# A two-layer graph network: the first attention's bias is added to X by the vector engine in the convolution's first 16 groups, instead of being multiplied in by the tensor engine

## What is computed

```python
xn = _layernorm(x)
x = x + gnn(xn, W, edge_index) + mix(xn, W_qkv, W_out, b_out)
# gnn: h = xn @ W; out = segment_sum(h[src] * norm, dst)
# mix: ... context = k^T v; out = (q @ context) @ W_out + b_out
```

## Time and profile before

| | |
|---|---|
| median of 3 runs | 2628.09 us |
| lowest, highest | 2627.09, 2628.97 us |
| span of the profiled execution, first to last instruction | 2779.7 us |
| the same less the median | 151.6 us |
| busy in that span: PE, PEld | 82%, 68% |
| DVE, ACT, POOL | 52%, 31%, 57% |
| gather stage, first to last gather | 138.3 to 1302.1 us |

### The profile page before, as it was taken

One profiled execution on the slowest core, in us unless ns is written; L12 is line 12 of the kernel. 1 busy time (PEld: TensorE's weight loads), 2 busy tenths in 40 slices (PEclk: granted clock), 3 DMA queues, 4 the chain that ended last, 5 costly groups with the idle time before them and its releaser, 6 DMA issues. The chain is left out here.

```text
span 2779.7 us, 48472 instructions
## 1 busy us (share of the span) xinstructions
PE 2272.5 (82%) x13041; PEld 1897.3 (68%) x13042; DVE 1437.7 (52%) x3979; ACT 857.8 (31%) x2513; POOL 1598.0 (57%) x2187
## 2 busy tenths in 40 slices
PE   7854767767677676665979999999998999996898
PEld 5633555555455554343869999978888999995798
DVE  9742534333444445336752222258876777777211
ACT  2500222222112111112623333346663434432333
POOL 4666566665666666674035555458866555552232
PEclk9977878777787787667599999999999999998899
DMA  5233233332333333332323334332221111111121
GB/s 156 98 98 89 77 88 88 87 91 78 89 91 88 89 91 90 90 94 70 127 78 104 102 124 135 106 89 87 79 68 54 45 43 42 45 43 63 29 35 31
DMA packets 138623, 227.41 MB, mean 82 GB/s; under 512 B 26651, under 2 KB 99056, under 8 KB 138546
## 3 DMA queue, kind: packets, MB, share of 16 engines
q0 software_dynamic: 56240, 142.70, 18.4%
q1 hardware_dynamic: 81186, 82.10, 8.9%
q10 hardware_dynamic: 1120, 1.71, 0.2%
HBM read 175.10 MB, written 51.30 MB: 81 GB/s over the span
## 5 line engine op out<-in xcount | busy, mean ns | idle before, releaser
L944 POOL DMA_INDIRECT all_XN<-h_table,l_srcI x782 | 774.7, 991 | 395.6 <-issue 217.0
L1145 PE MATMUL gcn_acc<-all_XN,gcn_hot 128*128 128x256 f32 x796 | 258.1, 470 | 96.0 <-DVE all_X L1036 45.3
L1145 PE MATMUL gcn_acc<-all_XN 128*128 128x256 f32 x768 | 249.5, 473 | 92.0 <-issue 41.3
L1145 PEld LDWEIGHTS gcn_acc<-all_XN,gcn_hot 128*128 128x128 f32 x796 | 178.7, 235 | 157.9 <-issue 77.3
L1145 PEld LDWEIGHTS gcn_acc<-all_XN 128*128 128x128 f32 x768 | 172.7, 236 | 149.8 <-issue 90.1
L878 ACT COPY gcn_seen_sb<-gcn_seen 128x392 f32<-128x392 f32 x98 | 47.4, 484 | 591.1 <-remote 489.6
L1836 ACT ACTIVATE moe_hidden<-moe_hid_ps,moe_b 128x128 f32<-128x128 f32 x420 | 131.2, 363 | 283.1 <-PE moe_hid_ps L1917 272.5
L1036 DVE SCALAR_TENSOR_TENSOR all_X<-gcn_acc,all_XN,all_X 128x256 f32 x392 | 170.3, 475 | 89.5 <-remote 81.5
L1917 PEld LDWEIGHTS moe_hid_ps<-moe_xst,held_held 128*128 128x128 f32 x1680 | 204.4, 193 | 11.9 <-issue 7.3
L1917 PE MATMUL moe_hid_ps<-moe_xst,held_held 128*128 128x128 f32 x1680 | 207.8, 277 | 1.9 <-DVE moe_xst L1857 1.9
L1924 PE MATMUL moe_y_ps<-held_held,moe_hidden 128*128 128x256 f32 x840 | 199.7, 381 | 0.8 <-DVE moe_y L1888 0.8
(11 more groups left out here) (431 smaller groups left out, 4737.2 us busy)
## 6 DMA issues: line engine op xcount, KB each, us to landing
held_held<-in_e_w SPq DMA_DIRECT2D x32, 512.0 KB
slots_out<-moe_y SPq DMA_DIRECT2D x105, 128.0 KB
all_XN<-h_table,l_srcI POOLq DMA_INDIRECT x782
all_X<-in_x SPq DMA_DIRECT2D x7, 896.0 KB, 11.2
rows_table<-all_XN SPq DMA_DIRECT2D x7, 896.0 KB, 4.2
z_table<-held_held SPq DMA_DIRECT2D x49, 128.0 KB, 1.9
x_table<-all_XN SPq DMA_DIRECT2D x49, 128.0 KB, 1.7
out<-all_X SPq DMA_DIRECT2D x49, 128.0 KB
```

The source lines that it names most:

```text
L944: nc.gpsimd.indirect_dma_start(msg[b][:, c, :], None, self.h_table, bass.IndirectOffsetOnAxis(self.srcI[:, GE * g + c:GE * g + c + 1], 0)) ...
L1145: last = nc.tensor.matmul(acc[b % NA][:, :], hot[b % NH][:, c, :], msg[b][:, c, :], start=(c == 0), stop=(c == n - 1))
```

## The change

DVE adds `b_out`, loaded once to all 128 partitions, to X in 16 pieces of 3 tiles (the last has 4), one behind each of groups 0 to 15, and waits for each to be complete. PE's product of ones by `b_out` goes, and so do its wait for `b_in` and SP's wait for `ctx_ready`: SP issues the load third in the stage, ahead of the two loads of W_q and W_out. In the wide groups T is added to all counts, so that they are positive: the table word `off` holds T more, and the semaphores start T higher.

```diff
+            BT = T // (CHUNKED * NB)
-            b_out = self.W0[0:1, 0, D:2 * D]
+            b_all = s.sb("b_all", [P, D])
...
-                            off = wide_word(eng, g, 2, -T, G * T)
+                            off = wide_word(eng, g, 2, 0, (G + 1) * T)
...
+                    sp.dma_start(b_all[:, :], spread(io["l0_vecs"][0:1, :], P)).then_inc(b_in, 16)
                     sp.dma_start(wq_t, io["l0_wq_t"]).then_inc(w_in, 16)
                     sp.dma_start(w_out, io["l0_w_out"]).then_inc(w_in, 16)
                     sp.wait_ge(tile_no_in, 32)
                     sp.wait_ge(w_in, 32)
-                    sp.wait_ge(ctx_ready, 1)
-                    sp.dma_start(b_out, io["l0_vecs"][0:1, :]).then_inc(b_in, 16)
                     sp.wait_ge(b_in, 16)
...
-                    link(nc.vector.tensor_tensor(wide_tab[:, :, 2], tiles[:, :], tile_f[0:1, 0, :], ALU.subtract))
+                    link(nc.vector.scalar_tensor_tensor(wide_tab[:, :, 2], tiles[:, :], float(T), tile_f[0:1, 0, :], ALU.add, ALU.subtract))
...
+                    def add_bias(g):
+                        end = T if g == CHUNKED * NB - 1 else BT * (g + 1)
+                        after(dve, b_in, 16)
+                        after(dve, added, 2 * (g - LAG + 1))
+                        x = X[:, BT * g * D:end * D].rearrange("p (t d) -> p t d", d=D)
+                        nc.vector.tensor_tensor(x, x, b_all[:, :].unsqueeze(1).broadcast_to([P, end - BT * g, D]), ALU.add).then_inc(b_added, 1)
+                        dve.wait_ge(b_added, g + 1)
...
                     for g in range(CHUNKED * NB):
                         turn(g // NB, g % NB)
+                        add_bias(g)
                         if 2 <= g < NC + 2:
                             chunk(g - 2)
...
+                    for ready in (wide_base, wide_hot, wide_added):
+                        dve.sem_inc(ready, T)
                     wide_groups(dve, add_wide, n_groups)
...
-                    pe.sem_inc(wide_summed, 1)
+                    pe.sem_inc(wide_summed, T + 1)
...
                         for b in range(KB):
-                            nc.tensor.matmul(sides[p][:, 0:D], xt[p][:, b, :], self.M[:, b, :], start=(b == 0), stop=False)
-                        nc.tensor.matmul(sides[p][:, 0:D], self.ones[0:1, :], b_out, start=False, stop=True).then_inc(add_done, 1)
+                            last = nc.tensor.matmul(sides[p][:, 0:D], xt[p][:, b, :], self.M[:, b, :], start=(b == 0), stop=(b == KB - 1))
+                        last.then_inc(add_done, 1)
...
                     pe.wait_ge(ctx_chain, 6)
-                    pe.wait_ge(b_in, 16)
                     pe.sem_inc(add_done, 1)
```

More of the change, by code:

```diff
@@ L792, in gather_stage @@
             b_in = s.sem("b_in")
+            b_added = s.sem("b_added")
             chunk_done = s.sem("chunk_done")
```

## The result

The changed kernel takes 2633.31 us in the median of 20 runs (2628.23 to 2641.22), the kernel before, run beside it, 2628.86 (2625.61 to 2634.81). The ratio is 1.0013, 95% interval 1.0007 to 1.0019: slower by 3.4 us (1.8 to 5.0) by the ratio, the two medians are 4.45 us apart. That is within what was called no change. Forecast were 2631.5 us and 3.4 us slower.

The account below looks back on a forecast made before the run. POOL issuing 782 gathers back to back was taken to bound the gather stage; all terms were 0 except the additions' hold on POOL: 2628.1 + 3.4 = 2631.5 us, range 2617 to 2644.

Parts of the forecast that it names:

- Gathers back to back bound the stage: Gather stage, timed run: lasts as long as POOL issues 782 gathers, 1013 us, plus a tail of some 10 us.
- The stops belong to the profiling: PE's stops of 1.87 us between products of one `see` come from profiling; the timed execution has next to none.
- the two numbers that agreed: 150.8 us, POOL's waits gone without PE's stops, against 151.6 us, profiled span over the timed median.
- PE's products are worth 0: Gather stage: PE loses 49 products of ones, 36.4 us busy, hidden under POOL's 5.2 us a group; worth 0 when timed.
- the rival: PE bounds the timed run too, the stops being real: 38 us gained, about 2590 us; chance 0.10.
- The wait for `b_out` is worth 0: PE's step behind the copy of M: that copy, not the load with its 6.4 us to land, ended the wait.
- DVE's 15.5 us are hidden: Groups 0 to 15: 16 additions raise DVE's work from 3.2 to 4.4 us of a 5.2 us group; worth 0.
- The additions hold POOL, +3.4 us: Groups 0 to 15: gathers starting under two-SBUF-input additions are held; +3.4 us, ends 0 and 13 us.
- The sign named for it: If right, gathers average longer than 0.987 us in the first 100 starts and are unchanged later.
- The formula: Mean hold of POOL per 0.953 us addition, starts 1.25 us apart: 0.27 us; 4.6 us in all, scaled by 35/47.
- The rule on two SBUF inputs: Skill: such DVE instructions contend with POOL's SBUF reads; its inference sparing descriptor generation would make the term 0, time 2628.1.
- The shift of DVE's work in groups 80 to 143 has no sign: Adds and one-hots move against gather starts as PE's attention steps shorten by 0.7 us; some 6 us either way, taken as 0.

Follow-up runs that it names:

- fast chips: Chips of the result and the last eight follow-up kernels; the kernel before takes 2627.28 or 2631.3 us there, 2628.86 beside the result.
- the slow chip: Chip on which the first four follow-up kernels ran; the kernel before takes 2773.22 us there (35 runs, none profiled).
- the extra tile: In PE's part alone (no products of ones, first attention's bias left out), experts get one tile more; 2776.69 us on the slow chip, 1.0018.
- the two variants that keep PE's products: Against the kernel before, DVE's 16 additions with PE's product kept: bias counted twice, 2636.5 us (1.0042); or PE multiplying zeros, 2633.72 us (1.0007).
- the counts alone: Kernel before with only the wide groups' changed counts, PE's products of ones kept: 2630.66 us, ratio 1.0000 (0.9991 to 1.0009).
- the pair of 48 additions: Kernel before with changed counts plus 48 unused 128x768 additions, groups 144 to 191; second input in SBUF 2652.18 us (1.0082), PSUM 2630.05 (0.9995).

## Why the prediction was right, point by point

- *Gathers back to back bound the stage.* Right on the fast chips, and seen in their profiles: 1017.7 us from first to last gather against the 1013 worked out.
- *The stops belong to the profiling.* Wrong, though the forecast didn't suffer, which was luck: had the times come from the slow chip, the additions would have cost nothing there (0.9996). This is the step that failed: "I take from this that the stops belong to the profiling". On the slow chip executions without a profile take 2773 us, and profiles on fast chips have no stop. The profile of before, with its span of 2779.7 us and POOL's 172.2 us of waits, looks like those of the slow chip (profiled spans from 2765.6 to 2773.9, times of the kernel before up to 2782.5), and the times shown came from a fast one. Its chip is not on record, so this is inferred. By it the two numbers that agreed, 150.8 and 151.6, measured the difference of two chips. The Trainium skill ("NOTIFIC — the notification-queue block", 7.1 Overflow) says that the block's inner stages hold a producer back rather than lose a record; no run here shows that it did, and the changed kernel's profiled execution, with 48320 instructions, took 2633.71 us where the median is 2633.31. The shortening of the profiled span by 20 to 40 us, which followed from the step, did not come; it was 148.
- *PE's products are worth 0.* Right, also on the slow chip, where the rival looked best: with the products gone and POOL waiting for PE there was no gain (1.0018, with about 3.9 us of it the extra tile). POOL still waited 134.5 us for PE, so these products are not what holds PE there.
- *The wait for `b_out` is worth 0.* In the changed kernel PE's next step begins at 570.7 us, right behind the copy of M (569.9 to 570.5), as in the earlier trace rows. Right.
- *DVE's 15.5 us are hidden.* Right: no wait of POOL beyond 0.3 us behind the first gather. The instruction takes about 950 ns, 953 were worked out.
- *The additions hold POOL, +3.4 us.* Right in kind and size: 3.7 us read off the gathers that meet them, 3.4 (1.8 to 5.0) in time. That it is 3.4 to the tenth is luck: the same 16 additions met 10 and 12 gathers in the two variants that keep PE's products and cost 4.4 and 5.4 us there, and the work displaced behind them added some more. The sign named for it came: the first 100 gathers take 1.033 us in the mean, the later ones 0.992, against 1.000 and 0.994 with the counts alone. The formula is right for one instruction alone and too low for chains, where it missed half (21 us instead of 10 to 13).
- *The rule on two SBUF inputs* ("SBUF — State Buffer", Who interferes with whom, in the Trainium skill). It says that a DVE instruction with two SBUF inputs contends with a GpSimd instruction that reads SBUF; the pair of 48 additions agrees, with 22 us. The inference beside it, that tensor_tensor leaves descriptor generation alone, fails for these indirect gathers. That it is their reading of the row numbers that is held, as the prediction argued, no run here shows.
- *The shift of DVE's work in groups 80 to 143 has no sign.* The gathers there took 9.6 us over the plain 0.946 in the changed kernel and 10.7 with the counts alone. But over all profiles of fast chips it is 8.0 to 10.8 in the five kernels with PE's products and 7.2 to 11.0 in the four without, so no shift by the change is shown. It stayed within the 6 us allowed.

## What to carry to other kernels

Before asking what a faster engine is worth, find whose instruction list runs without waits: that list's length is the time of the stage, and only what lengthens or shortens it counts. Check first that the profile and the times can be of the same chip: their difference of 151.6 us was the warning here. If that list issues indirect DMAs from GpSimd, read the second input of every vector instruction that runs beside it: in SBUF it held the issue here, in PSUM it did not. Let a test variant keep the numbers, or count the work that depends on them.

## What the runs showed of the hardware that was not expected

**A chip on which PE stands still.** On the slow chip PE pauses, by up to 1.9 us at a time in this stretch, between products that wait for nothing the profile shows, while gathers go on, and here it works without a gap once POOL has paused. The stretch around the stop of the earlier trace rows, before, at and behind POOL's pause (PE, PEld, DVE, ACT, POOL busy with counts, clock, DMA share, GB/s):

```profile
1090.00:1100.50 10.50, 2.75 (x7) 1.34 (x7) 0.88 (x2) 0.00 (x0) 7.69 (x9) 0.50 0.35 100
1100.50:1103.00 2.50, 0.86 (x4) 0.41 (x4) 0.00 (x0) 0.00 (x0) 0.00 (x0) 0.50 0.19 52
1103.00:1109.00 6.00, 6.00 (x16) 4.73 (x16) 5.16 (x12) 2.89 (x6) 4.60 (x5) 0.51 0.22 66
```

7 products in 10.5 us, then 16 in 6 us. Whether the gathers cause the pauses was not tried, and what PE lacks stays open. The kernel before takes 145 us more on this chip than in the result's runs (2773 against 2628).

**Half of PE's saved time went into slower products.** In the 325 us from 545 to 870 PE's granted clock is 0.86 with the products of ones (counts alone) and 0.81 in the change. The clock alone does not follow the products, though: it is 0.81 or 0.82 in all four kernels of fast chips without them, and 0.81, 0.84, 0.86, 0.86 and 0.89 in the five with them. The sums' groups from 545 to 890 us, counts alone, then the change:

```profile
L1147 PE MATMUL gcn_acc<-all_XN 128*128 128x256 f32 x282 | 82.8, 444 | 34.4 <-DMA all_XN<-h_table,l_srcI 32.1 <-DVE gcn_hot L1027 2.4
L1147 PE MATMUL gcn_acc<-all_XN,gcn_hot 128*128 128x256 f32 x256 | 78.4, 459 | 34.5 <-DMA all_XN<-h_table,l_srcI 31.9 <-DVE all_X L1036 2.6
...
L1186 PE MATMUL gcn_side<-l_W,all_ones 1*128 1x256 f32 x50 | 18.6, 453 | 0.0
L1186 PE MATMUL gcn_tab<-l_W,all_ones 1*128 1x256 f32 x48 | 17.0, 433 | 0.0
```

```profile
L1157 PE MATMUL gcn_acc<-all_XN 128*128 128x256 f32 x283 | 90.1, 473 | 44.9 <-DMA all_XN<-h_table,l_srcI 36.3 <-DVE all_X L1037 6.7 <-DVE all_XN L1028 1.8
L1157 PE MATMUL gcn_acc<-all_XN,gcn_hot 128*128 128x256 f32 x256 | 84.1, 485 | 41.6 <-DMA all_XN<-h_table,l_srcI 38.2 <-DVE all_X L1037 3.4
```

35.6 us of products go, the sums take 13.0 us more at the lower clock, and PE's idle time before them grows by 17.6 us. PE's busy time from 545 to 890 us falls by 17.5 us only (273.4 to 255.9). Neither part shortens the stage: PE waits for the same gathers.
